# Attention in units of 256 queries, the scores of two steps in a row, three score buffers

## What is computed

```python
x = x + attention(layernorm(x))      # 32 query heads, 8 key/value heads, head size 64, softmax(q k^T / 8) v, then Wo and bo
h = layernorm(x)                     # feed-forward part: 8192 inner columns, integer weights with a scale for each row
x = x + (silu(h @ Wg.T) * (h @ Wu.T)) @ Wd.T
```

## Time and profile before

| | |
|---|---|
| median of 3 runs | 2057.16 us (2057.03 to 2139.9) |
| profiled execution, its own time | 2057.45 us |
| its span on the slowest core (3) | 2055.9 us |
| spans of the 8 cores | 2052.0 to 2055.9 us |
| mean granted TensorE clock | 0.996 to 0.999 of 2.4 GHz |
| TensorE busy | 2020.7 us (98%) |
| ScalarE busy / VectorE busy | 1082.9 us (53%) / 1017.4 us (49%) |

### The profile page before, as it was taken

How to read it: one execution, slowest core, us unless ns; L and a number is a source line. 1 busy time by engine, 2 the same in 40 slices (tenths; PEclk the granted TensorE clock), 3 DMA queues, 4 the chain that set the end, 5 groups by cost and what they waited for, 6 DMA issues and landing times.

```text
span 2055.9 us, 27559 instructions; the slowest of 8 cores (2052.0 to 2055.9 us)
## 1 busy us (share of the span) xinstructions
PE 2020.7 (98%) x9616; PEld 835.8 (41%) x9616; DVE 1017.4 (49%) x1265; ACT 1082.9 (53%) x1203; POOL 124.5 (6%) x177
## 2 busy tenths in 40 slices
PE   5999999999999999999999999999999999999999
PEld 3543222223333335444444444444444444444444
DVE  5623666665655657666666666666666102020202
ACT  2325999998888873554444454544444332333230
POOL 2000111101000100000000000000000000000000
PEclk9999999999999999999999999999999999999999
DMA  9528433332332527655555445544554857464661
GB/s 235 182 42 151 90 62 72 62 57 52 67 67 56 109 63 234 135 113 103 104 112 116 90 84 92 91 83 84 93 91 83 211 118 163 82 144 82 121 121 45
DMA packets 47364, 213.97 MB, mean 104 GB/s; under 512 B 5888, under 2 KB 5888, under 8 KB 30080
## 3 DMA queue, kind: packets, MB, share of 16 engines
q0 software_dynamic: 20160, 134.23, 38.7%
q1 hardware_dynamic: 27072, 77.98, 11.7%
HBM read 319.14 MB, written 27.26 MB: 168 GB/s over the span
## 4 chain that ended last, share of the span: by engine, by line
PE 97%; DMA 1%; DVE 1%; ACT 0%; issue 0%; DVEq 0%; ACTq 0%; SPq 0%; POOLq 0%
PE PS_C L166 26%; PE PS_B L166 24%; PE PS_A L166 21%; PE PS_D L166 12%; PE PS_C L162 8%; PE PS_B L162 3%; PE PS_A L162 2%; PE PS_D L162 1%; PE PS_D L177 1%; DMA arena<-wv 1%; DMA arena<-xt 0%; DVE arena L200 0%; ACT arena L187 0%; DVE bns L200 0%; PE PS_D L174 0%
## 5 line engine op out<-in xcount | busy, mean ns | idle before, releaser
L166 PE MATMUL PS_C<-arena 128*128 128x512 bf16 x2202 | 602.8, 382 | 0.1
L166 PE MATMUL PS_B<-arena 128*128 128x512 bf16 (+1 forms) x2156 | 550.5, 381 | 0.3 <-DVE arena L200 0.3
L187 ACT ACTIVATE arena<-arena 128x1024 bf16<-128x1024 bf16 x384 | 379.5, 1046 | 289.7 <-DMA arena<-dwt 289.7
L166 PE MATMUL PS_A<-arena 128*128 128x512 bf16 (+2 forms) x1948 | 500.9, 382 | 10.9 <-DMA arena<-wv 6.9
L187 ACT ACTIVATE arena<-PS_B 128x1024 bf16<-128x1024 f32 (+1 forms) x288 | 281.1, 976 | 279.4 <-PE PS_B L162 273.8
L166 PEld LDWEIGHTS PS_B<-arena 128*128 128x128 bf16 (+1 forms) x2156 | 209.6, 97 | 332.5 <-issue 109.5
L166 PEld LDWEIGHTS PS_C<-arena 128*128 128x128 bf16 x2202 | 214.7, 98 | 309.6 <-issue 104.1
L166 PEld LDWEIGHTS PS_A<-arena 128*128 128x128 bf16 (+1 forms) x1948 | 190.2, 98 | 316.0 <-issue 124.2
L166 PE MATMUL PS_D<-arena 128*128 128x512 bf16 x1108 | 316.4, 380 | 0.0
L200 DVE TENSOR_TENSOR arena<-PS_A,arena 128x512 f32<-128x512 f32 (+1 forms) x108 | 75.4, 698 | 454.6 <-PE PS_A L162 454.6
L200 DVE TENSOR_TENSOR arena<-arena 128x1024 bf16<-128x1024 bf16 (+2 forms) x436 | 290.9, 682 | 11.3 <-ACT arena L187 3.6
(11 more groups left out here) (46 smaller groups left out, 858.3 us busy)
## 6 DMA issues: line engine op xcount, KB each, us to landing
arena<-gwt POOLq DMA_DIRECT2D x32, 1024.0 KB, 9.3
arena<-uwt POOLq DMA_DIRECT2D x32, 1024.0 KB, 9.4
arena<-dwt POOLq DMA_DIRECT2D x32, 1024.0 KB, 9.5
arena<-xt SPq DMA_DIRECT2D x16, 1024.0 KB, 13.1
arena<-wq POOLq DMA_DIRECT2D x32, 512.0 KB, 7.1
arena<-wo POOLq DMA_DIRECT2D x6, 2048.0 KB, 21.4
arena<-xt SPq DMA_DIRECT2D x32, 256.0 KB, 5.9
x2d<-arena SPq DMA_DIRECT2D x32, 256.0 KB, 5.7
```

What stands on the lines that cost most here:

```text
L166: e.matmul(o, ll, rr, start=a, stop=b, skip_group_check=k))
L187: e.activation(o, i, f, bias=b, scale=s)
```

## The change

- A unit is one pair of heads with 256 queries: 64 units of 8 steps, 512 steps as before. A step takes 256 keys: `scores(n)` issues four matmuls with 64 rows and 256 columns (two blocks of 128 keys, two heads), `context(n)` four of 128 rows and 256 columns. The exponential of a step is 128x1024 as before.
- The main loop issues two steps' scores one behind the other, then the context of about two earlier steps (`ctx_steps`: 1, 3, 2 and 2 in the four rounds of a unit), then the filler: about 320 matmuls in rounds 4 to 127 and 384 in rounds 128 to 255.
- The scores go to `PS_A`, `PS_B` and `PS_C` in turn. The context of both heads adds up in one bank of `PS_D`; the filler has the other bank alone, so that a tile waits for the tile just before it.
- `divide` is cut in three parts, one in each following round; the copy stands right behind the last context. Q tiles may run two groups ahead (`QT` has three buffers).
- Behind attention the order of the PSUM tensors in `PS3` is turned round and some waits get new numbers.

```diff
         def QT(grp, i):
-            return bfv((162 + 4 * (grp % 2) + i) * KB, 512)
+            return bfv(((162, 166, 198)[grp % 3] + i) * KB, 512)
...
         def q_first(k):
             t_wait(*wd_wq[k])
-            if k >= 2:
-                t_wait(DVE, dve_q[k - 2])
+            ps = half(PS_C if k < 2 else PS_D, k)
...
+        CT_BANK = half(PS_D, 0)
+        FILL_BANK = half(PS_D, 1)
         def scores(n):
-            u, kc = divmod(n, 16)
+            u, st = divmod(n, 8)
...
-            ps = (PS_A, PS_B)[n % 2]
+            ps = (PS_A, PS_B, PS_C)[n % 3]
...
-            t_wait(ACT, act_e.get(n - 2, 0))
+            t_wait(ACT, act_e.get(n - 3, 0))
...
-            mm(ps[:, 0:512], KT(j2)[0:64, kc * P:(kc + 1) * P],
-               QT(grp, i)[0:64, :], start=True, stop=True)
-            mm(ps[:, 512:1024], KT(j2)[64:128, kc * P:(kc + 1) * P],
-               QT(grp, i)[64:128, :], start=True, stop=True, inc=True)
+            for k2 in range(2):
+                kc = 2 * st + k2
+                for hh in range(2):
+                    r = slice(64 * hh, 64 * hh + 64)
+                    mm(ps[:, hh * 512 + k2 * 256:hh * 512 + k2 * 256 + 256],
+                       KT(j2)[r, kc * P:(kc + 1) * P],
+                       QT(grp, i)[r, qq * 256:qq * 256 + 256],
+                       start=True, stop=True, inc=(k2 == 1 and hh == 1))
...
+        def context(n):
...
+            for k2 in range(2):
+                for hh in range(2):
+                    c = hh * 512 + k2 * 256
+                    mm(CT_BANK[:, hh * 256:(hh + 1) * 256],
+                       V128(2 * st + k2)[:, (2 * j2 + hh) * P:
+                                         (2 * j2 + hh + 1) * P],
+                       PT(n)[:, c:c + 256],
...
+            if st == 7:
+                v_wait(PE, pe_x[n])
+                v_wait(DVE, dve_nm.get(u - 4, 0))
+                dve_ct[u] = v_op("tensor_copy", CTU(u), CT_BANK, inc=True)
...
         def fill_bank():
             k = fill_n[0]
             fill_n[0] += 1
-            if k >= 2:
-                t_wait(DVE, fill_free[k - 2])
-            return k, half(PS_D, k)
+            t_wait(DVE, fill_free[k - 1] if k else dve_q[3])
+            return k, FILL_BANK
...
+        def ctx_steps(k):
+            n = [2 * k - 3, 2 * k - 2]
+            if n[1] % 8 == 0:
+                n = n[:1]
+            if n[0] % 8 == 1:
+                n = [n[0] - 1] + n
+            return [m for m in n if 0 <= m < 512]
...
+        for k in range(258):
+            for n in (2 * k, 2 * k + 1):
+                if n < 512:
+                    scores(n)
+            if k == 0:
+                q_first(2)
+                q_first(3)
...
+            for n in ctx_steps(k):
+                context(n)
+                if n % 8 == 7:
+                    todo += [(n // 8, p) for p in range(3)]
+            if k in count:
+                i_, c_ = count[k]
+                if i_ not in run:
+                    kind, t = FILL[i_]
...
+                    run[i_] = q_tile(t) if kind == "Q" else w_tile(t)
+                for _ in range(c_):
+                    next(run[i_])
+            if todo:
+                divide(*todo.pop(0))
...
-        PS3 = [PS_A, PS_B, PS_C]
+        PS3 = [PS_C, PS_B, PS_A]
```

More of the change, by code:

```diff
@@ L248, in QT, with CTU, REC @@
         def QT(grp, i):
-            return bfv((162 + 4 * (grp % 2) + i) * KB, 512)
-        def CTU(u):
-            return f32v((170 + 4 * (u % 2)) * KB, 1024)
-        REC = f32v(178 * KB, 1024)
+            return bfv(((162, 166, 198)[grp % 3] + i) * KB, 512)
+        def CTU(h):
+            return f32v((170 + 2 * (h % 4)) * KB, 512)
+        def REC(h):
+            return f32v((178 + 2 * (h % 2)) * KB, 512)
         BOB = f32v(182 * KB, D)
@@ L461, in q_first @@
             t_wait(*wd_wq[k])
-            if k >= 2:
-                t_wait(DVE, dve_q[k - 2])
+            ps = half(PS_C if k < 2 else PS_D, k)
             for c in range(16):
-                q_mm(k, c, half(PS_C, k))
-            q_ev(k, half(PS_C, k))
+                q_mm(k, c, ps)
+            q_ev(k, ps)
             g_wait(PE, pe_q[k])
@@ L479, in ld_wo @@
                                                 bfv(kb * KB, II), wo[n, :, :]))
-        units = [(qh, pj) for qh in range(2) for pj in range(16)]
+        units = [(qh, pj, qq) for qh in range(2) for pj in range(16)
+                 for qq in range(2)]
         act_e, pe_s, pe_x, dve_ct, dve_nm = {}, {}, {}, {}, {}
-        XSCHED = {4: [0], 5: [1, 2], 6: [3], 7: [4, 5]}
-        for s_ in range(8, 18):
-            XSCHED[s_] = [s_ - 2]
+        CT_BANK = half(PS_D, 0)
+        FILL_BANK = half(PS_D, 1)
         def scores(n):
-            u, kc = divmod(n, 16)
-            qh, pj = units[u]
+            u, st = divmod(n, 8)
+            qh, pj, qq = units[u]
             j2, i = divmod(pj, 4)
-            grp = u // 4
-            ps = (PS_A, PS_B)[n % 2]
+            grp = u // 8
+            ps = (PS_A, PS_B, PS_C)[n % 3]
             if n == 0:
-                t_wait(DVE, dve_0)
+                t_wait(DVE, max(dve_0, dve_q[1]))
                 t_wait(ACT, act_0)
-            t_wait(ACT, act_e.get(n - 2, 0))
-            if kc == 0 and i % 2 == 0:
+            t_wait(ACT, act_e.get(n - 3, 0))
+            if st == 0 and qq == 0 and i % 2 == 0:
                 t_wait(DVE, dve_q[4 * grp + 1 + i])
-            mm(ps[:, 0:512], KT(j2)[0:64, kc * P:(kc + 1) * P],
-               QT(grp, i)[0:64, :], start=True, stop=True)
-            mm(ps[:, 512:1024], KT(j2)[64:128, kc * P:(kc + 1) * P],
-               QT(grp, i)[64:128, :], start=True, stop=True, inc=True)
+            for k2 in range(2):
[6 more added lines that the diff above has]
+                       start=True, stop=True, inc=(k2 == 1 and hh == 1))
             pe_s[n] = C['pe']
@@ L510, in scores @@
             act_e[n] = s_act(PT(n), ps[:], AF.Exp, scale=0.125, inc=True)
-        def context(u, kc):
+        def context(n):
+            u, st = divmod(n, 8)
             j2 = units[u][1] // 4
-            n = 16 * u + kc
             if n == 0:
@@ L517, in context @@
             t_wait(ACT, act_e[n])
-            if kc == 0:
+            if st == 0:
                 t_wait(DVE, dve_ct[u - 1] if u else dve_q[3])
[L520 to L524, removed]
-            pe_x[n] = C['pe']
[L527 to L535, removed]
+            for k2 in range(2):
[5 more added lines that the diff above has]
+                       PT(n)[:, c:c + 256],
+                       start=(st == 0 and k2 == 0 and hh == 0),
+                       stop=(st == 7 and k2 == 1),
+                       inc=(k2 == 1 and hh == 1), skip=True)
@@ new lines, in context, with divide @@
+            pe_x[n] = C['pe']
+            if st == 7:
+                v_wait(PE, pe_x[n])
+                v_wait(DVE, dve_nm.get(u - 4, 0))
+                dve_ct[u] = v_op("tensor_copy", CTU(u), CT_BANK, inc=True)
+        dve_rc = {}
+        def divide(u, part):
+            qh, pj, qq = units[u]
+            if part < 2:
+                cs = slice(part * 256, part * 256 + 256)
+                if part == 0:
+                    v_wait(DVE, max(dve_ct[u], dve_nm.get(u - 2, 0)))
+                dve_rc[u] = v_op("reciprocal", REC(u)[0:64, cs],
+                                 CTU(u)[64:128, cs], inc=True)
+                return
+            v_wait(DVE, dve_rc[u])
@@ L536, in divide @@
             for hh, h in enumerate(_heads_of_pair(pj)):
-                cs = slice(hh * 512, hh * 512 + 512)
+                cs = slice(hh * 256, hh * 256 + 256)
                 b = (h % 2) * 64
[L539 to L542, removed]
+                dve_nm[u] = v_op(
+                    "tensor_mul",
+                    CTXT(qh, h // 2)[b:b + 64, qq * 256:qq * 256 + 256],
+                    CTU(u)[0:64, cs], REC(u)[0:64, cs], inc=True)
@@ L621, in ld_xr @@
             if tm == 5:
-                y_wait(DVE, dve_nm[31])
+                y_wait(DVE, dve_nm[63])
             if tm in XR_PREV:
@@ L641, in w_tile @@
             t_wait(*wd_wo[n])
-            t_wait(DVE, dve_nm[15])
+            t_wait(DVE, dve_nm[31])
             for dc in range(16):
@@ L668, in w_tile @@
                 yield
[L670 to L685, removed]
+        FILL = [("Q", k) for k in range(4, 24)]
+        k_, w_ = 24, 0
+        for c_ in "QQWQQWWQWQWQWQWWWWWWWWWW"[:24]:
+            if c_ == "Q":
+                FILL.append(("Q", k_))
+                k_ += 1
+            else:
+                FILL.append(("W", w_))
+                w_ += 1
+        assert (k_, w_) == (32, 16)
+        share = {}
+        for i_ in range(20):
+            a_, b_ = 4 + i_ * 124 // 20, 4 + (i_ + 1) * 124 // 20
+            share[i_] = list(range(a_, b_))
+        for i_ in range(24):
+            a_, b_ = 128 + i_ * 128 // 24, 128 + (i_ + 1) * 128 // 24
+            share[20 + i_] = list(range(a_, b_))
+        def ctx_steps(k):
```

(35 more changed lines are left out.)

## The result

| | before | after |
|---|---|---|
| median | 2057.1 us (4 runs) | 2026.24 us (4 runs) |
| profiled execution / its span | 2057.45 / 2055.9 us | 2026.54 / 2025.0 us |
| ratio to before, 95% interval | | 0.985 [0.983, 0.987] |

1.5% faster; 2023 us was forecast.

What follows compares the result with a forecast made beforehand. TensorE's own list was taken to bound attention: 335.2 pieces + 151.9 fillers + 8.8 + 1.1 + 54.3 switches + 15.9 bank stalls = 567.2 us against 601.9, gain 34.7, so 2023 us; forecast range 2010 to 2036 (chance 0.57).

Steps and rivals of the forecast that it cites:

- What bounds the kernel: Attention: nothing but TensorE's own list sets the time; it waits once, for 1.1 us in 591 us.
- Switches: Attention rounds on TensorE: two steps share one change to 64 rows and one back; gain 54.3 us.
- Pieces of 256 columns: Attention scores and context: 3072 matmuls of 256 columns in place of 1536 of 512; loss 3.7 us.
- The 11 us more for pairs behind pairs: Scores: possible extra 0.014 us behind every pair following a pair, 768 times; taken as 0.
- Filler in one bank: Filler tiles in attention: first matmul waits until the tile before is emptied; loss 15.9 us, bounds 0 and 28 more.
- The rival that the wait is covered: Filler bank in attention: emptying is quicker or tiles' ends fall well; gain 50.6 us, 2007 us; chance 0.15.
- ScalarE with three buffers: Scores buffers in attention: ScalarE needs 1.84 us a round against TensorE's 2.08 or 2.17; cost 0.
- Start, end, DMA at 0: Attention's first rounds, its end and Q weight loads four tiles ahead stay as now: cost 0, start give or take 2 us.

Runs made afterwards that it cites:

- the two-buffer runs: Two steps' scores in a row in the kernel before: 2037.6 us, ratio 0.991; changed kernel with two score buffers, third tensor for the filler: 2041.3 us, 0.992.
- the run without the wait: Changed kernel with the first two loads of output projection weights asked for in round 40: 2023.0 to 2023.5 us, ratio 0.983.
- The run of the pieces alone: Kernel before with each attention matmul of 512 columns cut into two of 256, same weights: ratio 1.0016; profiled execution 2064.65 us.
- moving four lines: Changed kernel with the filler ahead of the context in a tile's last round, where it has two or three context steps: 2011.4 to 2012.4 us, ratio 0.978.

## Why the prediction was right

*What bounds the kernel* held: every experiment moved the time by what it put into TensorE's list or took out, matmuls, switches or waits.

*Switches.* 54.3 us forecast for 256 rounds. Undoing them cost 43.6 us of attention, plus some 6 of bank stalls which the extra switches cover (by the working put on record), plus the 3.5 of the `wq` wait that is missing there: 53 us, 0.207 a pair of switches. By the starts, a round of the changed kernel without a wait is 0.213 us longer than its streams, whether it has one, two or three steps of context, where 0.212 was taken from the kernel before.

*Pieces of 256 columns.* 3.7 forecast, 3.3 (1.2 to 5.3) measured alone. The 11 us more for pairs behind pairs, which the prediction weighed, did not come.

*Filler in one bank.* 15.9 forecast. By the starts, the stall at the first matmul of a tile behind a Q tile is in nearly all cases 0.95 us with one step of context, 0.52 with two and 0.08 to 0.22 with three (forecast 0.99, 0.55, 0.12), in 8, 11 and 9 rounds as forecast. These (15.7) and the W tiles (1.3) come to 17.0 us, and taking most of them away gave 13.7 us of attention. The rival that the wait is covered falls.

*ScalarE with three buffers.* Cost 0 forecast, and apart from 0.8 us at the start there is no wait for it. The forecast needed no rule for the size of such a wait; the rule on record for the two-buffer runs was wrong by half.

*Start, end, DMA at 0.* This is the term that failed. Its loads were taken as early enough because the issue order stayed. The kernel before was nearer to a wait than that: on its slowest core the load of 37 us lasted 35, landed at 206.7, and the tile's first matmul starts at 208.96, 2.3 us later. The changed kernel is ready for that matmul at 206.0 (its start in the run without the wait), and the weights landed at 208.0: 3.7 us, with the slow clock behind. The pace is not all of it. The run of the pieces alone, which is no faster than the kernel before, waited on three of its cores, by 4.9 us on the one where this load took 42 us; on the others it took 33 to 38. So a margin of 2 us was inside the spread of landing times. The wait is most of the 5 us by which attention exceeded its forecast (572.2 against 567.2); the bank's stalls were 1.1 over theirs, and 0.3 is a delay of VectorE told of below.

That the profiled execution is only 3.7 us over its forecast, and not 5, is luck: 1.0 us comes from an earlier start of attention, which lies at 163.4 to 165.4 us on the cores of the kernel before.

Two rules of the Trainium skill (page "TensorE: Matmul & The Clock Gate") had been weighed: an estimated 107 ns for a load of 128 columns ("LDWEIGHTS (loading the stationary operand)"), and a load under a running matmul only where the row groups differ ("The mechanism"). The traces differ from both, and they decide: 128x128 loads, each with its matmul, repeat every 55.7 ns, and the pairs here are 0.11 us apart, each with new weights in the same rows as the pair before, so both loads of a pair are hidden in this case.

## What to carry to other kernels

When one engine is never idle, look at the starts in its own list: here a change between 64-row and 128-row matmuls cost 0.1 us each way, 1024 times, while the page showed 98% busy. Group work of one kind as far as the buffers go, and work out the wait for a buffer as a loop: what went out before the wait runs during it, so a shortfall costs half in a round of this kind (on average: single rounds waited much more or not at all). Then ask of each buffer given up what now stands behind its wait, and whether the order can put cover there: moving four lines was worth 13.7 us, nearly half of what the whole change brought. And check the landing times of loads against the new pace and against their spread over cores and runs, not against one trace of the old kernel.

## What was not expected of the hardware

- A switch between row modes shows no idle time in the profile; the weight loads and the matmul simply start 0.1 us late.
- Behind TensorE's stop of 2.7 us for `wq`, in the middle of steady work, the granted clock fell to 0.50 (1.2 GHz) for some 3 us, which cost 1.4 us beside the 2.1 us that the wait added to its own round. The same drop followed on three more cores, which had stopped for 3.2 to 3.55 us; on the other four, which had stopped for 1.75 to 2.4 us, the clock stayed at 2.4 GHz.
- In the changed kernel two multiplications of 64x256 on VectorE took 2.56 us in place of 0.75, while GpSimd's two additions of 128x512 ran from 559.40 to 561.90. It delayed the context bank by 0.3 us. It is no single case: on the eight cores 41 of the 1024 multiplications of this shape begin while such an addition runs, and each of them ends some 0.29 us behind the end of the addition (0.42 us is usual), or of two additions in a row. The 7 that began first kept their 0.42 us. The 55 copies out of PSUM and the 117 reciprocals that begin inside an addition are no longer than the others (0.69 and 1.75 us). So these multiplications wait for GpSimd's addition; what it is that they share no run here shows. VectorE's row, then GpSimd's:

```profile
559.97 2.56 DVE L200 TENSOR_TENSOR arena<-arena 64x256 bf16<-64x256 f32 x2
```

```profile
559.40 2.50 POOL L208 TENSOR_TENSOR arena<-arena 128x512 f32<-128x512 f32 x2
```
